# The argument of tanh in a recurrence: from the state memory into the accumulator bank

## The reference

```python
def cell(h, x):
    gi = x @ W_ih + b_ih
    gh = h @ W_hh + b_hh
    i_r, i_z, i_n = jnp.split(gi, 3, axis=-1)
    h_r, h_z, h_n = jnp.split(gh, 3, axis=-1)
    r = jax.nn.sigmoid(i_r + h_r)
    z = jax.nn.sigmoid(i_z + h_z)
    n = jnp.tanh(i_n + r * h_n)
    h_new = (1.0 - z) * n + z * h
    return (h_new, h_new)
...
x = x + _L0_cond_ref(x, cond_2048[:, None, :], ...)
x = x + _L1_cond_ref(cond_2048, x, ...)
```

## Time and profile before

| | before |
|---|---|
| median of three runs | 2276.47 us (2275.55 to 2278.33) |
| the profiled execution, its own time | 2284.52 us |
| its span | 2282.4 us |
| granted TensorE clock, mean | 0.992 |
| PE, PEld, DVE, ACT, POOL busy | 96%, 75%, 55%, 51%, 9% |

### The profile page before, as it was taken

The page is one execution under the profiler, slowest core; times in us unless marked ns, Lnnn a source line. Parts: engine busy times, 40 slices in busy tenths (PEclk is TensorE's granted clock), DMA queues, the critical chain, the costliest instruction groups (busy, mean ns, idle before and its releaser), DMA issues.

```text
span 2282.4 us, 129581 instructions
## 1 busy us (share of the span) xinstructions
PE 2181.6 (96%) x58384; PEld 1704.1 (75%) x58384; DVE 1253.8 (55%) x4464; ACT 1153.2 (51%) x4603; POOL 202.6 (9%) x223
## 2 busy tenths in 40 slices
PE   5999999999799999999999999999999999999998
PEld 3655656556478888888888888888888888888776
DVE  2664656646535555555555555555555555555554
ACT  2664746646334454544545454554545454554544
POOL 4314233143200000000000000000000000000000
PEclk9999999999999999999999999999999999999999
DMA  6000000000110000000000000000001000000000
GB/s 212 1 1 19 2 19 1 2 1 1 56 41 23 17 26 18 27 18 27 20 22 28 17 27 19 26 18 27 22 20 30 17 28 17 28 19 23 26 5 13
DMA packets 41081, 54.99 MB, mean 24 GB/s; under 512 B 9424, under 2 KB 34000, under 8 KB 40528
## 3 DMA queue, kind: packets, MB, share of 16 engines
q1 hardware_dynamic: 34112, 38.81, 5.4%
q0 software_dynamic: 1584, 7.73, 0.9%
q10 hardware_dynamic: 4832, 0.15, 0.1%
HBM read 29.90 MB, written 16.78 MB: 20 GB/s over the span
## 4 chain that ended last, share of the span: by engine, by line
PE 85%; DVE 5%; ACT 4%; POOL 2%; issue 2%; DMA 1%; POOLq 1%; ACTq 1%; SPq 0%; DVEq 0%
PE ps L457 56%; PE ps L304 8%; PE ps L443 7%; PE ps L355 5%; PE ps L378 4%; PE ps L392 2%; DVE znT L778 2%; PE ps L430 2%; ACT xb L624 2%; DVE xb L789 2%; ACT z_trip L621 2%; POOL qk_rs L284 1%; POOLq L62 1%; DMA wqkv<-in_L_cond_W_hh 0%; POOL norm_qk L286 0%
## 5 line engine op out<-in xcount | busy, mean ns | idle before, releaser
L457 PE MATMUL ps<-wqkv,xb 128*4 128x128 f32 x49152 | 1480.1, 273 | 40.7 <-DVE xb L789 29.2
L457 PEld LDWEIGHTS ps<-wqkv,xb 128*4 128x4 f32 x49152 | 1224.5, 87 | 280.1 <-DVE xb L789 227.9
L621 ACT ACTIVATE z_trip<-znT 128x8 f32<-128x8 f32 x1024 | 219.0, 214 | 369.5 <-DVE znT L778 369.5
L789 DVE TENSOR_TENSOR_SCAN xb<-z_trip,xb 128x24 f32<-128x24 f32 x1024 | 213.3, 208 | 291.7 <-ACT xb L624 291.7
L794 DVE STREAM_TRANSPOSE rT<-ps 128x128 f32<-128x128 f32 x512 | 162.2, 317 | 346.9 <-PE ps L457 346.9
L778 DVE STREAM_TRANSPOSE znT<-ps 128x128 f32<-128x128 f32 x1024 | 313.1, 306 | 67.7 <-PE ps L457 6.8
L615 ACT ACTIVATE r_pair<-rT 128x16 f32<-128x16 f32 x512 | 112.4, 219 | 436.9 <-DVE rT L794 436.9
L443 PE MATMUL ps<-wih,x1T 128*32 128x256 f32 (+1 forms) x4096 | 240.2, 328 | 0.0
L624 ACT ACTIVATE xb<-v_pair 128x16 f32<-128x16 f32 x1024 | 222.8, 218 | 12.6 <-DVE v_pair L783 0.7
L783 DVE TENSOR_TENSOR_SCAN v_pair<-r_pair,znT 128x16 f32<-128x16 f32 x1024 | 196.1, 192 | 35.6 <-DVE znT L778 0.8
L583 ACT ACTIVATE probs<-ps,negmax 128x512 f32<-128x512 f32 x256 | 172.7, 686 | 69.2 <-DVE negmax L701 69.2
(11 more groups left out here) (76 smaller groups left out, 985.6 us busy)
## 6 DMA issues: line engine op xcount, KB each, us to landing
gi_spill<-gi_image SPq DMA_DIRECT2D x64, 192.0 KB, 2.1
seeds<-gi_spill SPq DMA_DIRECT2D x228, 32.0 KB
seeds<-gi_spill SPq DMA_DIRECT2D x284, 16.0 KB
xb<-in_x SPq DMA_DIRECT2D x4, 1024.0 KB, 5.6
out<-xb SPq DMA_DIRECT2D x64, 64.0 KB, 2.1
wqkv<-in_L_cond_W_qkv SPq DMA_DIRECT2D x1, 3072.0 KB, 11.9
wih<-in_L_cond_W_ih POOLq DMA_DIRECT2D x1, 3072.0 KB, 14.7
wqkv<-in_L_cond_W_hh POOLq DMA_DIRECT2D x1, 3072.0 KB, 10.5
```

The source lines that it names most:

```text
L457: last = nc.tensor.matmul(ps[QD * j:QD * j + B, bank, 0:P], hist_flat[:, first:first + 3 * B - 2:3], weights, start=False, stop=False, ski ...
L621: nc.scalar.activation(z_trip[:, 8 * half:8 * half + 8, 2], znT[:, half, 0:16:2], ACT.Sigmoid).then_inc(s[z_name], 1)
L789: return nc.vector.tensor_tensor_scan(next_elements(step, half), z_trip[:].rearrange("p e s -> p (e s)")[:, 24 * half:24 * half + 24], ele ...
```

## The change

The scan of `candidate` writes its 16 places into columns 256 to 271 of the bank from which its own half's sums came (bank `zna` for half a, `znb` for half b, of this step's parity), and tanh reads from there. `v_pair` goes. No instruction is added or removed, and none changes its place in the order of its engine; shapes, steps of the patterns and waits are the same.

```diff
-        v_pair = sb("v_pair", [P, 16, 2])
...
+        def arguments(step, half):
+            return ps[:, step_banks(step)[1 + half], 2 * P:2 * P + 16]
...
                     act.wait_ge(s[v_name], step + 1)
                     nc.scalar.activation(elements(step, half).rearrange("p (e s) -> p e s", s=3)[:, :, 0:3:2],
-                                         v_pair[:, 8 * half:8 * half + 8, 1].unsqueeze(2).broadcast_to([P, 8, 2]),
+                                         arguments(step, half)[:, 1:16:2].unsqueeze(2).broadcast_to([P, 8, 2]),
                                          ACT.Tanh).then_inc(s[n_name], 1)
...
                 def candidate(half):
                     first = 16 * half
                     return nc.vector.tensor_tensor_scan(
-                        v_pair[:].rearrange("p e s -> p (e s)")[:, first:first + 16],
+                        arguments(step, half),
                         r_pair[:].rearrange("p e s -> p (e s)")[:, first:first + 16],
                         znT[:, half, 16:32], 0.0, ALU.mult, ALU.add)
```

## The result

The changed kernel takes **2259.97 us** (median of 4 runs, 2258.14 to 2262.77) beside 2276.81 us for the kernel before, run on the same chip. The ratio is 0.9927 with a 95% interval of 0.991 to 0.9944: 16.8 us faster, where 34.8 were forecast. The profiled execution took 2261.02 us with a span of 2258.8, at the same mean clock (0.992).

A forecast was written before the change was run, and what follows sets the result against it. The prediction took a loop of latencies through both halves, 3.14 us per step, as the bound. Tanh's -34.8 us plus 0 for the scan took the median from 2276.5 to 2241.7 us, range 2211 to 2291.

The forecast's parts named there:

- the loop of latencies: Per step, DVE, ACT and PE wait in turn through both halves: 3.14 us, 1608 us over 512 steps.
- I take 0 ns, by the memset: Candidate scan on DVE: writing into the bank costs nothing; ends from 11 ns gain to 48 ns loss.
- the write costs more than the read saves: Rival at the scan's end, which releases tanh: 14 ns net loss per pair, 14.3 us slower; chance 0.22.
- I take 34 ns: Tanh on ACT: reading from the bank saves 34 ns, 34.8 us over 1024 runs; other end 53 ns.
- What covers, and what is late next: Neighbours of the loop on PE, DVE and ACT: none takes the gain; PE keeps 0.12 us idle before half b.
- PE takes one half of it: Rival: PE's array runs late, half a gains nothing, only half b counts; 17.4 us faster, 2259.1 us; chance 0.08.
- The range of the forecast alone: Total time if tanh is 34 ns shorter and the scan about as long: 2222 to 2260 us; chance 0.50.

The follow-up runs named there:

- the write alone: Against the changed kernel, tanh reads a constant tile in the state memory while the scan still writes into the bank; 2286.86 us, ratio 1.0027 to the kernel before.
- the light pair: Changed kernel and kernel before, both without seed refills and without the input side of the gates in the recurrence; 2248.12 and 2272.51 us.
- the read alone: Against the changed kernel, the scan writes to the state memory as before and tanh reads 16 constant bank columns; 2263.55 us, ratio 0.9935 to the kernel before.
- scan twice: Changed kernel with each candidate scan run twice, first into unused columns of the same bank; 2334.90 us, ratio 1.0245 to the kernel before.

## Why the prediction was wrong

The sign, the place and the mechanism of the loop held. The regular step shows every link: the loop of latencies through both halves, tanh released by the scan, two pairs per step with no cover. The size failed, at two steps: a term of the sum (8 us; tanh's 2 ns less than forecast are 2 us more) and the cover, where PE's stops were priced at nothing (7 to 10 us).

- **"I take 0 ns, by the memset"** is the term of the sum that was mis-sized. The write costs 8 ns (192 to 200, in the changed kernel and in the write alone), 8 x 1024 = 8.2 us. The memset's equal rows in both memories didn't carry over to a scan; why a scan pays and a memset doesn't, no run here shows. The figures of the Trainium skill (Perfetto Trace Analysis, Optimizing Scalar/DVE Operations) had the sign of this term right and its size wrong (65 ns more by their difference, 8 measured). For tanh they give 42 ns less, and 32 were measured. So the rival that the write costs more than the read saves, slower by 14.3 us by the rows and by 23.6 by those figures, fell: 8 ns against 32.
- **"I take 34 ns"** for tanh held: 32 measured. L563, the copy that waits for its producer, gave the right number and L604, with 53, didn't; that the waiting is what makes the difference wasn't tested. Both terms together give 24 ns per pair and 24 us, and the light pair of kernels shows 24.4.
- **"What covers, and what is late next"** is the other step that failed. It took PE's slack per step from the timeline of a regular step and found that it would suffice. On a regular step it does: the regular steps came out within 2 ns of what the two prices give. But PE's loads stop now and then for 0.1 to 0.8 us with no semaphore to wait for, and the prediction priced no such stop. The slack in front of PE was 0.12 + 0.15 us in the step of the earlier trace rows, one with a piece of 16 loads; each ns off the loop came out of it. Of 24 us in the regular steps the medians show 14 to 17, and of 33 us in the read alone 18: three to five tenths of the gain are lost in the irregular steps. Of the 8 us that the write alone adds they show 5, which the noise can't tell from 8.
- The rival **"PE takes one half of it"** had the number (2259.1) and named the right engine with the wrong mechanism. It expected half a to gain nothing in every step. In fact both halves gained in every regular step, and the loss sits in the steps that are over 30 ns longer: 73 and 51 before, 69 and 89 in the changed kernel, 92 in the read-only one. That its number fits is luck.
- **The range of the forecast alone** (2222 to 2260) reached the result only with its very end, and the range on record (2211 to 2291) held it. The steps named there as wrong if seen (scan longer by over 34 ns, tanh shorter by less than 10, step still 3.14) weren't seen.

That PE's stops are what gives the gain back is shown from two sides: more room at the same PE work (scan twice), and less PE work at the same pace (the light pair) both leave no stop and under 5 us above the regular step, and in the light pair the medians show the full gain. What stops PE is, by the places and times of the 291 stops, the supply of its instructions; it isn't shown by a run that changed the supply alone. Why only some packets come too late, 29 and 42 of the 415 in the changed kernel, stays open. The transfers of the seeds aren't the whole reason: without them there are still 28 there, and 14 in the kernel before. It wasn't tried either whether DVE's evacuations, which went with the light pair's PE work, have a share; in the scan-twice kernel they were all there, and the stops were gone.

No whole version here beats the changed kernel: `r_pair` in a bank gives 2 ns per scan and no time.

## What to carry to other kernels

Price an operand's move from the row that is most alike in form and in how it starts (here a waiting copy came within 2 ns for a waiting tanh), and don't take a memset for the price of a write by arithmetic. In a loop of latencies, compare the regular step and the time above it separately: a change can earn its full price in the regular step and give a third of it or more back in irregular ones. When an engine beside the loop has only 0.1 to 0.3 us of room per step, its rare stops are the next bound. Look at where in its stream they lie before you look for their cause, and seek the next gain in that engine's work; here the medians showed the whole 24 us once the pieces of the input side were left out.

## What the runs showed of the hardware

- ACT on a small tile (128x16): reading from the accumulator memory saves 32 ns (tanh 218 to 186), writing to it 31 ns (sigmoid of r 219 to 188). DVE on the same size: writing there costs a scan 8 ns (192 to 200), and reading one operand there saves 2 (200 to 198).
- With tanh reading from the bank, the instructions behind it show longer. The seed copies, which weren't touched, went from 263 to 276 ns and from 368 to 380, and did so in each kernel whose tanh reads from the bank (276 or 277, and 380), but not in the write-alone kernel (263 and 368):

```profile
L601 ACT ACTIVATE ps<-seeds 128x256 f32<-128x256 f32 x512 | 194.5, 380 | 0.0
...
L600 ACT ACTIVATE ps<-seeds 128x128 f32<-128x128 f32 x512 | 141.1, 276 | 51.1 <-DMA seeds<-gi_spill 51.1
```

  L600 now starts 0.08 us behind tanh's start (1503.43 to 1503.51 in ACT's timeline) where it was 0.12. It is off the path, and costs nothing here.
- PE stops more often the denser its work: 22 to 54 stops per execution at regular steps from 3.159 down to 3.079 us, and none once a step has 0.17 us more (scan twice) or one piece of work less. The stops lie at places 127.36 loads apart, one for each 16384-byte packet of instructions, and end 1.19 to 1.63 us behind the end of a packet.
